# A graph layer with a screened second layer on one Trainium2 core: the engines' orders behind the support stage written out tile by tile, other gathered tiles, and another queue for the half chunks

## The reference, cut to what matters

```python
h = relu(layernorm(x))                        # x: 2048 x 512
xq = round(min(h / aa, 1) * 15)               # integers 0 to 15
wq = round(|clip(w_norm / wa, -1, 1)| * 7) * sign
support = relu(xq @ wq * deltas)              # 2048 x 512
s = round(min(support / aa2, 1) * 15)         # integers 0 to 15
x1 = x + (adj @ s) * scale                    # adj: 2048 x 2048, f32
h2 = relu(layernorm(x1))
out = x1 + attention(h2)                      # scores are masked: only where adj == 1, and the diagonal
```

## Time and profile before

| what | us |
|---|---|
| median of 3 runs | 169.4 (167.04 to 170.91) |
| the profiled execution, its own time | 167.91 |
| its span | 166.1 |
| busy: PE / DVE / ACT / POOL | 124.7 / 114.2 / 96.0 / 77.7 |
| support stage ends, TensorE starts tile 4 | 67.20 |
| last result computed, VectorE | 161.21 |

### The profile page before, as it was taken

The page is one execution under the profiler, slowest core; times in us unless marked ns, Lnnn a source line. Parts: engine busy times, 40 slices in busy tenths (PEclk is TensorE's granted clock), DMA queues, the critical chain, the costliest instruction groups (busy, mean ns, idle before and its releaser), DMA issues.

```text
span 166.1 us, 1981 instructions
## 1 busy us (share of the span) xinstructions
PE 124.7 (75%) x578; PEld 74.0 (45%) x582; DVE 114.2 (69%) x245; ACT 96.0 (58%) x145; POOL 77.7 (47%) x115
## 2 busy tenths in 40 slices
PE   0599998399985988999994059999369959969200
PEld 0584454155542533475663025656126525659200
DVE  0999994478997599599992058833493493887770
ACT  3797777148883974779000799912991991911100
POOL 2546235057073288000078793885675576261110
PEclk9999999969999999999999858999969978999965
DMA  5999999826968999958462168833232142111121
GB/s 173 348 409 412 412 393 388 76 48 221 225 189 251 270 319 404 381 183 347 39 253 79 42 236 275 275 135 98 77 129 66 63 132 73 63 63 67 63 82 52
DMA packets 18288, 32.45 MB, mean 195 GB/s; under 512 B 7841, under 2 KB 10658, under 8 KB 16738
## 3 DMA queue, kind: packets, MB, share of 16 engines
q1 hardware_dynamic: 16306, 26.38, 47.7%
q10 hardware_dynamic: 1008, 3.54, 6.6%
q0 software_dynamic: 960, 2.36, 4.7%
HBM read 24.66 MB, written 6.30 MB: 186 GB/s over the span
## 4 chain that ended last, share of the span: by engine, by line
POOL 27%; DVE 26%; issue 18%; DMA 12%; PE 8%; ACT 4%; ACTq 0%; DVEq 0%; POOLq 0%
DMA h_iT<-h_i 10%; POOL raw L815 8%; POOL narrow L827 8%; POOL rs L734 7%; DVE st L1007 4%; PE acc L1328 4%; DVE ring L1114 3%; POOL ring L845 3%; DVE x_sb L1258 3%; DVE most L1064 3%; DVE sup L1052 3%; ACT h_i L565 2%; DMA w_sb<-weight 2%; DVE h_qT L1047 2%; DVE sup_h L1051 1%
## 5 line engine op out<-in xcount | busy, mean ns | idle before, releaser
L1395 PE MATMUL acc<-sup_h,hi 128*128 128x512 f16 (+1 forms) x144 | 34.4, 399 | 13.1 <-ACT hi L538 13.0
L1401 PE MATMUL acc<-sup,lo 128*128 128x512 f32 (+1 forms) x144 | 32.3, 377 | 1.3 <-DVE lo L1107 1.3
L734 POOL TENSOR_TENSOR rs<-ve,minus_half 128x1 f32<-128x1 f32 (+2 forms) x21 | 19.5, 927 | 20.4 <-DVE ve L1017 20.2
L1395 PEld LDWEIGHTS acc<-sup_h,hi 128*128 128x128 f16 x144 | 14.6, 107 | 31.7 <-ACT hi L538 14.9
L1401 PEld LDWEIGHTS acc<-sup,lo 128*128 128x128 f32 x144 | 24.9, 189 | 6.6 <-DVE lo L1107 1.6
L1107 DVE TENSOR_TENSOR lo<-raw,hi 128x2048 fp32r<-128x2048 f32 x7 | 16.8, 2401 | 10.8 <-ACT hi L538 10.8
L546 ACT ACTIVATE junk<-raw,below 128x2048 uint8<-128x2048 f32 x12 | 23.9, 1989 | 0.1
L1346 PE MATMUL acc<-sup,lo 128*128 128x512 f32 x64 | 22.6, 466 | 0.5 <-DVE sup L1052 0.5
L815 POOL DMA_INDIRECT raw<-adj_g,at_sb x12 | 13.9, 1156 | 19.3 <-DMA at_sb<-at_d 16.3
L1114 DVE SCALAR_TENSOR_TENSOR ring<-ring,rs,x_sb 128x512 f32<-128x512 f32 x11 | 8.3, 756 | 18.7 <-POOL rs L734 12.9
L1328 PE MATMUL acc<-w_q,h_qT 128*128 128x512 bf16 x60 | 16.0, 387 | 6.9 <-DVE h_qT L1047 6.5
(11 more groups left out here) (121 smaller groups left out, 170.3 us busy)
## 6 DMA issues: line engine op xcount, KB each, us to landing
raw<-adj_t SPq DMA_DIRECT2D x11, 1024.0 KB, 6.7
out<-ring SPq DMA_DIRECT2D x15, 256.0 KB, 2.0
x_sb<-x SPq DMA_DIRECT2D x3, 1024.0 KB, 14.5
raw<-adj_t SPq DMA_DIRECT2D x4, 512.0 KB, 14.8
raw<-adj_t ACTq DMA_DIRECT2D x4, 512.0 KB, 5.1
sup_d<-sup_h SPq DMA_DIRECT2D x4, 512.0 KB
w_sb<-weight SPq DMA_DIRECT2D x4, 258.0 KB, 4.0
raw<-adj_t ACTq DMA_DIRECT2D x1, 1024.0 KB, 5.7
```

What stands on the lines that cost most here:

```text
L734: nc.gpsimd.tensor_tensor(rs[:, a:a + m], ve[:, a:a + m], minus_half[:, 0:m], ALU.pow).then_inc(r_ready, 1)
L1395: nc.tensor.matmul(bank[:, cols], part(hi, k % PARTS, j), sup_h[:, j, cols], start=(j == 0), stop=False)
L1401: ins = nc.tensor.matmul(bank[:, cols], part(lo, k % PARTS, j), sup[:, j, cols], start=False, stop=(j == T - 1))
```

## The change

SPARSE becomes (9, 11, 13, 15): tiles 9, 11, 13 and 15 are gathered, and 4 to 8, 10, 12 and 14 are dense. There are still eight dense tiles and twelve screened chunks. The last tile, which is worked in two halves, is now a gathered one. The loops over s are gone; ScalarE, VectorE, GpSimd and SyncE have their orders written out. The first four tiles are treated as all others (`relu2`, `result`), and GpSimd's scaling and subtracting for them is gone. The first four half chunks are no longer issued by SyncE ahead of everything else but by ScalarE at j = 4 to 7, the second four by ScalarE at j = 11 to 14 (they were issued at 12 and 13); `flag_half(2)` to `flag_half(7)` stand at j = 11 to 16 on VectorE, one for each j (before: two at 11, none at 12, one each at 13 to 16). SyncE issues all loads ahead of all stores. The diff, cut to its core:

```diff
-SPARSE = (8, 10, 12, 14)
+SPARSE = (9, 11, 13, 15)
...
@@ SyncE
-            for n in range(4):
-                load_half(sp, n)
...
-            nxt = GT + 5
-            for s in range(GT, T):
-                if nxt < ND:
-                    load_adj(nxt)
-                    nxt += 1
-                for t in (range(GT) if s == GT else [s - 1]):
-                    store(t)
+            for k in range(GT + 5, ND):
+                load_adj(k)
+            for t in range(T - 1):
+                store(t)
@@ ScalarE
                 if j <= T:
                     relu_sup(j - 1)
+                if j < 8:
+                    load_half(act, j - 4)
+                elif 11 <= j < 15:
+                    load_half(act, j - 7)
...
-                if j in (12, 13):
-                    for n in (2 * j - 20, 2 * j - 19):
-                        load_half(act, n)
...
-            for s in range(GT, T):
-                a, m = second_ln[s - GT]
-                if s + 2 < T and s + 2 not in SPARSE:
-                    split_hi(ordinal(s + 2))
-                elif s + 2 < T:
-                    split_high(SPARSE.index(s + 2))
-                    widen(SPARSE.index(s + 2))
-                if seen < ND:
-                    screen_ones(seen)
-                    seen += 1
-                for t in range(a, a + m):
-                    relu2(t)
+            split_hi(5)
+            screen_ones(2)
+            screen_ones(3)
+            split_hi(6)
+            screen_ones(4)
+            split_hi(7)
+            screen_ones(5)
+            split_hi(8)
+            screen_ones(6)
+            for t in range(GT):
+                relu2(t)
+            split_high(0)
+            widen(0)
+            split_hi(ordinal(10))
+            screen_ones(7)
+            relu2(4)
+            relu2(5)
...
@@ GpSimd
             gather_rows(0)
             gather_sup(0)
-            gathered = 1
-            for s in range(GT, T):
-                a, m = second_ln[s - GT]
-                pool.wait_ge(var_ready, FIRST - EARLY + 1 + s - GT)
-                inverse_root(a, m)
-                if s == GT:
...
-                    for t in range(GT):
-                        pool.wait_ge(yp_ready, t + 1)
-                        nc.gpsimd.tensor_tensor(ring[:, t % RING, :], ring[:, t % RING, :], x_sb[:, t, :],
-                                                ALU.subtract).then_inc(first_out, 1)
-                if gathered < S and SPARSE[gathered] - s <= 4:
-                    gather_rows(gathered)
-                    gather_sup(gathered)
-                    gathered += 1
-            assert gathered == S
+            second_root(0, GT)
+            gather_rows(1)
+            gather_sup(1)
+            second_root(4)
+            second_root(5)
+            gather_rows(2)
+            gather_sup(2)
+            second_root(6)
+            second_root(7)
+            gather_rows(3)
+            gather_sup(3)
+            for t in range(8, T - 1):
+                second_root(t)
@@ VectorE, in the support stage
-                if j == 11:
-                    flag_half(2)
-                    flag_half(3)
-                if 13 <= j < T + 1:
+                if j <= T - 1:
                     flag_half(j - 9)
+                elif j == T:
+                    flag_half(7)
@@ VectorE, behind it (residual: x_sb, statistics and ve of a tile)
+            split_lo(6)
+            residual(0, GT)
+            residual(4)
+            split_lo(7)
+            residual(5)
+            split_lo(8)
+            for t in range(GT):
+                result(t)
+            residual(6)
+            split_rest(0)
+            residual(7)
+            split_lo(ordinal(10))
+            result(4)
+            result(5)
+            residual(8)
+            split_rest(1)
+            result(6)
+            result(7)
+            residual(9)
+            split_lo(ordinal(12))
+            result(8)
+            residual(10)
+            split_rest(2)
+            residual(11)
+            split_lo(ordinal(14))
+            result(9)
+            result(10)
+            result(11)
+            residual(12)
+            split_rest(3)
+            residual(13)
+            count_row()
+            result(12)
+            result(13)
+            residual(14)
+            last_residual(T - 1)
+            result(14)
```

151 lines of the change are left out of this document (70 added, 81 removed).

## The result

| | before | changed | changed, measured again |
|---|---|---|---|
| median (lowest to highest), us | 169.84 (167.04 to 170.91) | 149.87 (148.40 to 154.65) | 150.43 (148.45 to 152.68) |
| executions | 4 | 4 | 6 |
| ratio to before, 95% interval | | 0.883 (0.856 to 0.910) | 0.893 (0.884 to 0.901) |
| profiled execution, us (span) | 167.91 (166.1) | 148.40 (146.6) | 148.45 (146.7) |

The forecast was 152 us (146.5 to 159). The range holds the time; the forecast is 2.1 us too high. Where it went is worked out in the part on why the prediction was right. The median of before is now of four executions, 169.84 us instead of the 169.4 of the first three.

What follows compares the result with a forecast made beforehand. Behind the support stage, engine handovers were taken to bind the kernel, with GpSimd setting the pace. The profiled 167.91 us less 13.4 (late part) and 3.4 (early part) gave 151.1, plus 1.0 for a median: 152 us, range 146.5 to 159.

Steps and rivals of the forecast that it cites:

- GpSimd's walk: GpSimd's gathers, roots and holds by VectorE's splits, from the first gather at 83.2 to the root of tile 8 at 125.1.
- the collisions: Four of VectorE's splits (tiles 7, 8, 10, 12) hold GpSimd up, 1.5 us each, 6.0 in all.
- The waits that come back: VectorE waits about 5 and 4 us for roots 6 and 8; TensorE idles 2.7 behind tile 12's split, again before tile 13's second part.
- The tail: After root 8 at 125.1 VectorE never waits again; its remaining work takes 22.7 us and ends at 147.8 instead of 161.2.
- The rival on TensorE's clock: TensorE's clock falls in both new stalls, about 1.9 us each, at most 2 us beyond the slack: 154 us; chance 0.08.
- Late stretch: Time from the start of the first gather to the end of the last result; forecast to end 13.4 us earlier.
- Early part: Support stage: moving the half chunks and spreading the reductions gains 3.4 us, between -0.7 and 6.1.
- The rival that they bring nothing: Moved half chunks still use the same DMA engines and gain nothing: 155.4 us; chance 0.2.
- The flags: VectorE's half-chunk reductions, one instead of two at j = 11, shorten TensorE's 1.68 us wait for h_qT: 0.8 us.
- 8.1 us stall ahead of tile 7: TensorE's idle time behind ScalarE's hi of tile 7; claimed gone, with its 1.9 us of slow clock.
- GpSimd slower than its rows: 18 later gathers each take 0.3 us longer beside VectorE's work, root 8 comes 5.4 later: 157.5 us; chance 0.12.
- ScalarE's queue held: Half-chunk issues at j = 4 to 7 hold ScalarE 4.29 us each, 17.2 in all: 176.6 us; chance 0.03.

Runs made afterwards that it cites:

- x8: The changed kernel with each of VectorE's 2048-column splits cut into four of 512: 144.42 us, ratio 0.852 to the kernel before.
- x7: The changed kernel with tile 14 gathered in place of 15, so the last tile is dense: 150.85 us, ratio 0.897 to the kernel before.
- x12: The changed kernel with the first four half chunks back in SyncE's queue, second measurement: 153.14 us, ratio 0.912 to the kernel before.
- x1: The changed kernel with the first four half chunks back in SyncE's queue: 153.36 us, ratio 0.908 to the kernel before.
- x2: The changed kernel with the flags and the last four half chunks back in their old places: 151.28 us, ratio 0.902 to the kernel before.
- x5: The kernel before with only ScalarE's split of chunk 7 and the screening behind it moved ahead of the first relu2: 168.39 us, ratio 0.998.
- x4: The changed kernel with GpSimd's roots of tiles 6 and 7 ahead of the third gather block, 8 and 9 ahead of the fourth: 146.70 us.
- x9: The changed kernel with both the roots moved ahead of gather blocks and VectorE's splits in four: 140.45 us, ratio 0.829 to the kernel before.
- x10: x9 with the load of one dense chunk moved from SyncE's queue to ScalarE's, one turn earlier: 140.69 us, ratio 0.829 to the kernel before.
- x6: The kernel before with the first four tiles finished like the others, without GpSimd's scaling and subtracting: 164.61 us, ratio 0.979.

## Why the prediction was right

**GpSimd's walk (right).** Root 8 was forecast 41.9 us behind the first gather, and is ready after 119.73 - 78.41 = 41.3. Part of this closeness is luck, since the terms were off in both directions: the collisions, taken at 1.5 each or 6.0, measured 6.9, and the 24 gathers with their pauses 30.6 instead of 30.1, but the roots took 3.9 instead of 5.8. Five single roots were counted at 0.93 each, as behind a wait; two in a row take 1.10 together. x8 shows that they are what the prediction read them as: standing still until the split is over.

**The waits that come back (right).** VectorE at results 6 and 8: about 5 and 4 us forecast, 5.29 and 5.33 measured. TensorE behind `lo` of tile 12: 2.7 forecast, 2.13 measured; behind `rest` of tile 13: 3.67.

**The tail (right, 1.1 us too long).** 22.7 forecast, 21.6 measured. I had used 1.87 us for a residual; when other work follows it, the next starts after 1.80 (122.89 to 124.69), and results in a row are 0.67 apart; the rest is 0.1 or 0.2 less for each `rest`, the split and the last tile. The rival on TensorE's clock came true for one of its two stalls: behind the wait of 2.13 us the 16 matmuls took 3.92 us at the full clock, behind that of 3.67 us the granted clock was 0.50 from 123 to 126, and `hi` of tile 14 took 4.38 us instead of 3.63. (In x7 it fell behind a wait of 2.14 us too: the 16 matmuls behind it took 5.53.) It cost nothing, because the slack at the end was larger: the products of tile 15 are done at 134.8 and VectorE asks for them at 137.2.

**Late stretch in sum.** 64.6 us forecast, 63.0 measured: 1.6 us, the whole of the tail's 1.1 and 0.5 of GpSimd's walk. The profiled execution was to take 151.1 us and took 148.4: 1.6 of the difference lie here, 1.4 ahead of the first gather, where that profile gained 4.8 instead of 3.4, and 0.3 go back behind the last result.

**Early part (right in size, split not wholly settled).** 3.4 us forecast; about 3 by what the late stretch leaves over. Of this the half chunks were to bring 2.6 (2.1 and 0.5 of slow clock) and bring 2.7 to 3.2 (x12) or 3.5 (x1). The rival that they bring nothing falls. The flags were to bring 0.8 and bring 0.4 to 0.8 or nothing (x2).

**What the text weighed wrongly.** The prediction's first paragraphs give the 8.1 us stall ahead of tile 7 and its 1.9 us of slow clock as what is lost there. x5 takes both away, and the late stretch gets 0.9 us shorter. The sum was not hurt, because it was made along GpSimd's walk and counted neither; but whoever had added the stall to the gain would have been 10 us off. The chain of before said it already: 8% on TensorE, 27% on GpSimd.

**Rivals.** GpSimd slower than its rows: no; of the 24 gathers 21 take 0.94 to 1.24 us, two stand under a split, and one takes 1.44 us beside `rest`. ScalarE's queue held: no, 0.373 us at most.

**Slips in the working.** The times at which VectorE wants tiles 14 and 15 (140.9 and 142.9) don't follow from the terms of the tail, which give 141.5 and 143.4, and the low end adds up to 146.3, not 146.5. Nothing hangs on either.

## What to carry to other kernels

A long idle time of the costliest engine is a gain only if it ends the chain: take it away by itself first, as x5 did, before the orders of all engines are rewritten around it. Walk the engine that ends the chain instruction by instruction, and count where another engine's long instruction holds it: cutting each of VectorE's splits in four (x8) and moving two pairs of roots each ahead of a block of six gathers (x4) brought 10 us more together (x9), half as much as the whole change before them. Where executions scatter in one stage, compare profiles by a stretch that begins behind it.

## What the runs showed of the hardware

- A GpSimd gather issue (indirect DMA) or a small power operation that begins beside VectorE's 128x2048 subtraction (`raw - hi`) ends only after it. Gathers took 1.99 to 3.05 us instead of 0.95 and ended 0.82 or 0.83 us behind the split (five cases in before and the changed kernel); the root of tiles 0 to 3 took 2.81 us instead of 1.06 and ended 0.91 behind it. Beside four 128x512 subtractions in a row a gather takes 0.95 to 1.45 us in x8, and up to 1.50 in x9 and x10.
- One case shows the same hold the other way round. In the kernel before GpSimd's last subtraction of the first tiles ends at 98.19, 0.96 us after a split has begun, and the split takes 3.12 us instead of 2.28:

```profile
97.23 3.12 DVE L1107 TENSOR_TENSOR lo<-raw,hi 128x2048 fp32r<-128x2048 f32 x1 [9.01 <-ACT hi L538]
```

- The same DMA transpose of 128 x 512 lands after 2.4 us or after up to 8.6 (both in x7) while bulk loads run. The first gather behind the ten transposes starts between 77.98 and 85.27 us in kernels whose support stage is the same or differs by one load.
- One of SyncE's four issues of a 512 KB load took 4.23 to 4.30 us in each of the five kernels that have them there (before, x1, x5, x6, x12), and none of ScalarE's eight, later ones took more than 0.373 in the changed kernel.
